# Joined: an alignment with blocks two slots apart and its teacher rows loaded early, and expert picks and most normalised rows made in the attention's tail

## The reference, cut to what matters

```python
x = x + _L0_xattn_ref(_layernorm(x), ctx, ctx, ...)      # 16 heads of 16, softmax attention
x = x + _L0_ffn_ref(_layernorm(x), W1, b1, W2, b2, Wr, br)  # mixture of 8 experts, top 1
x = x + _L1_xattn_ref(ctx, _layernorm(x))                # dynamic time warping (below)
x = x + _L1_ffn_ref(...)
x = x + _L2_xattn_ref(...)                               # attention
x = x + _L2_ffn_ref(...)                                 # mixture of 8 experts, top 2
x = x + _L3_xattn_ref(...)
x = x + _L3_ffn_ref(...)

# experts: logits = x @ Wr + br, the expert is their argmax, the gate a softmax of them
# warping, for each of 8 batches (teacher = ctx rows, student = normalised x rows):
D = sqrt(max(aa + bb - 2 * a @ b.T, 0))                  # 256 x 256 distances
R[i, j] = D[i, j] + min(R[i-1, j], R[i, j-1], R[i-1, j-1])
# walk back from R[255, 255] to R[0, 0] by the least neighbour;
# expanded[j] = sum of the teacher rows i that the path pairs with j
```

## Time and profile before

| | |
|---|---|
| median of 3 runs | 2441.24 us (2434.01 to 2441.58) |
| the profiled execution's own time | 2440.11 us |
| its span in the profile | 2438.3 us |
| busy: PE / PEld / DVE | 1987.9 (82%) / 1621.2 (66%) / 1604.2 (66%) |
| busy: ACT / POOL | 1183.1 (49%) / 951.7 (39%) |
| mean granted clock of PE | 0.825 |

### The profile page before, as it was taken

One profiled execution on the slowest core, in us unless ns is written; L12 is line 12 of the kernel. 1 busy time (PEld: TensorE's weight loads), 2 busy tenths in 40 slices (PEclk: granted clock), 3 DMA queues, 4 the chain that ended last, 5 costly groups with the idle time before them and its releaser, 6 DMA issues. The chain is left out here.

```text
span 2438.3 us, 40723 instructions
## 1 busy us (share of the span) xinstructions
PE 1987.9 (82%) x13441; PEld 1621.2 (66%) x13441; DVE 1604.2 (66%) x5274; ACT 1183.1 (49%) x3293; POOL 951.7 (39%) x919
## 2 busy tenths in 40 slices
PE   8985999599948967976999947777878778777888
PEld 5663898499937855655999935566656666665555
DVE  6776111588974237854111168999999999995786
ACT  3544232455421115543333325687777787875444
POOL 3311454300007023303555425666666666662210
PEclk9997999655779989987999965577777678757899
DMA  3112565520315012315354330000000000101442
GB/s 97 62 47 84 205 240 177 150 37 1 108 48 182 0 65 74 101 36 184 130 205 161 106 123 25 1 31 18 31 18 31 31 1 31 49 1 63 164 157 77
DMA packets 101861, 204.50 MB, mean 84 GB/s; under 512 B 20158, under 2 KB 70550, under 8 KB 93718
## 3 DMA queue, kind: packets, MB, share of 16 engines
q1 hardware_dynamic: 77568, 116.19, 14.3%
q0 software_dynamic: 23808, 85.50, 10.2%
q10 hardware_dynamic: 280, 0.23, 0.0%
HBM read 216.24 MB, written 55.28 MB: 111 GB/s over the span
## 5 line engine op out<-in xcount | busy, mean ns | idle before, releaser
L833 DVE MATCH_REPLACE8 l3a_left<-l3a_top,l3a_left 128x256 f32<-128x256 f32 x768 | 308.3, 409 | 0.0
L826 DVE MAX8 l3a_top<-l3a_left 128x8 f32<-128x256 f32 x768 | 285.5, 413 | 0.0
L525 POOL TENSOR_TENSOR l3a_prob<-l3a_expd,l3a_rest 128x512 f32<-128x512 f32 x128 | 162.8, 1272 | 211.4 <-ACT l3a_rest L608 210.4
L363 PEld LDWEIGHTS l3a_psO<-l3a_probT,l3a_vp 128*128 128x128 f32 x1024 | 185.5, 269 | 69.7 <-ACT l3a_probT L624 40.6
L363 PE MATMUL l3a_psO<-l3a_probT,l3a_vp 128*128 128x128 f32 x1024 | 210.0, 370 | 24.7 <-ACT l3a_probT L624 24.6
L345 PE MATMUL l3a_psT<-all_ident,l3a_prob 128*128 128x128 f32 x512 | 112.8, 361 | 106.0 <-POOL l3a_prob L525 105.2
L512 POOL TENSOR_TENSOR l3a_kept<-l3a_raw_sc,l3a_mone 128x512 f32<-128x512 f32 x128 | 163.7, 1279 | 71.9 <-ACT l3a_raw_sc L592 67.9
L2043 ACT ACTIVATE l2f_hT<-l2f_psH,l2f_wt 128x128 f32<-128x128 f32 x312 | 89.2, 369 | 209.8 <-PE l2f_psH L1997 209.8
L518 POOL TENSOR_TENSOR l3a_sc_sb<-l3a_kept,l3a_mlow 128x512 f32<-128x512 f32 x128 | 164.1, 1282 | 10.0
L345 PEld LDWEIGHTS l3a_psT<-all_ident,l3a_prob 128*128 128x128 f32 x512 | 80.0, 186 | 123.9 <-POOL l3a_prob L525 123.4
L2403 PE MATMUL dtw_psS<-dtw_r,all_shift 128*128 128x1 f32 x596 | 152.7, 356 | 10.2 <-DVE dtw_r L2583 9.8
(11 more groups left out here) (599 smaller groups left out, 4730.4 us busy)
## 6 DMA issues: line engine op xcount, KB each, us to landing
key_at<-l3a_a_k SPq DMA_DIRECT2D x8, 768.0 KB, 3.3
kv_at<-dtw_vd SPq DMA_DIRECT2D x8, 512.0 KB, 2.8
k_at<-dtw_kx SPq DMA_DIRECT2D x8, 512.0 KB, 4.2
l1f_kx<-k_at SPq DMA_DIRECT2D x8, 512.0 KB, 4.5
kv_at<-l1f_k SPq DMA_DIRECT2D x8, 512.0 KB, 3.2
l2a_k<-kv_at SPq DMA_DIRECT2D x8, 512.0 KB, 5.6
...
```

The costliest lines, as they stand in the source:

```text
L363: mm = nc.tensor.matmul(psO[y % 2][:, c, 0:P], vp[:, p, kc, c, g * P:g * P + P], probT[:, u % 2, kc, e, :], start=(j == 0 and e == 0 and k ...
L525: nc.gpsimd.tensor_tensor(prob[:, u % 4, :, :], expd[:, u % 2, :, :], rest[:, u % 2, :, :], ALU.subtract).then_inc(picked, 1)
L826: ins = nc.vector.max(top[:, e, eight], rows[:, e, :] if r else scores[:, e, :])
L833: ins = nc.vector.match_replace(out=rows[:, e, :], in_to_replace=top[:, e, eight], in_values=rows[:, e, :] if r else scores[:, e, :], imm_ ...
```

## The change

Five parts; the diff is cut to its core.

1. Attention tail (`l0a`, `l2a`): `routed(5)` is done before `out_project(6)` instead of after `values_apart(15)`, with two "spare" places in the bank order. ACT takes the roots there, in two groups (tiles 0 to 11, 12 to 15), and makes 12 of the 16 tiles of normalised rows; DVE makes `rstd`, the offsets and the picks of 12 tiles and then of 4; SP writes three of the four groups to `rows_x`.
2. `moe`: the roots, `max`, `max_index` and logits are gone from its start; `hot` is DVE's first work, four tiles of rows are left; two gathers are issued before the fourth fetch; 2 `keep_busy` instead of 4.
3. `Teacher`: the teacher rows (2 MB) and four turned batches (1 MB) are loaded during `l0f`, behind block 1's row copy, and their squares made on ACT behind the gelus of blocks 8 to 15.
4. `alignment`, front: moments in three groups (4, 4, 8 tiles), `minus_two(0)` and `(1)` before the third; no clearing of all of `d` and `r`; four `d2` buffers; 2 `keep_busy` at PE's start.
5. `alignment`, loop: `LAG` = 2, so `SLOTS` = 286. The scan takes its start value straight from PSUM, where PE's product is added onto columns that hold the large number for the first block; ACT is out of the loop. The scan writes 17 elements (row 0 of `r` too).

```diff
@@ paired_attention: turns, banks, PE
-                weighed = [("out", B - 2)] + weighed
+                weighed = ([("fl", B - 3), ("spare", 0), ("spare", 1)] if route is not None else []) + [("out", B - 2)] + weighed
...
-                if at >= 8:
-                    pe.wait_ge(reader[turns[at - 8][0]], turns[at - 8][1] + 1)
+                last = at - 8
+                if last >= 0 and turns[last][0] == "spare":
+                    last -= 8
+                if last >= 0:
+                    pe.wait_ge(reader[turns[last][0]], turns[last][1] + 1)
...
                 if y == 2 * B - 1 and t == 1:
+                    if route is not None:
+                        routed(B - 3)
                     out_project(B - 2)
@@ ACT
+            def row_roots(i):
+                a, z = PICKS[i]
+                act.wait_ge(r_moments, z)
+                nc.scalar.activation(r_std[:, a:z], mv[:, a:z, 1], ACT.Sqrt, bias=r_eps[:, 0:1]).then_inc(r_rooted, 1)
+            def rows_normalised(a, z):
+                for n in range(a, z):
+                    nc.scalar.activation(route["xn"][:, n, :], x[:, n, :], ACT.Identity, bias=route["offset"][:, n:n + 1],
+                                         scale=rstd[:, n:n + 1]).then_inc(r_norm, 1)
...
+                if route is not None and n == NQ + 5:
+                    act.wait_ge(r_eps_set, 1)
+                    row_roots(0)
+                if route is not None and n == NQ + 11:
+                    row_roots(1)
+                if route is not None and n == NQ + 9:
+                    rows_normalised(8, PICKS[0][1])
                 if route is not None and t == 3 and 0 <= (n - 15) // 4 < B:
                     read_rows((n - 15) // 4)
+                if route is not None and n == NQ + 6:
+                    act.wait_ge(r_off, 1)
+                    rows_normalised(0, 8)
@@ DVE
+            def row_scales(i):
+                a, z = PICKS[i]
+                dve.wait_ge(r_rooted, i + 1)
+                then(nc.vector.reciprocal(rstd[:, a:z], r_std[:, a:z]))
+                nc.vector.scalar_tensor_tensor(out=route["offset"][:, a:z], in0=mv[:, a:z, 0], scalar=-1.0, in1=rstd[:, a:z],
+                                               op0=ALU.mult, op1=ALU.mult).then_inc(r_off, 1)
+            def pick_experts(i):
...
+                dve.wait_ge(lg_ev, z // QT)
...  (lg * rstd, + br, max and max_index of tiles a to z)
+                if route is not None and n == NQ + 13:
+                    pick_experts(1)
                 if n == NQ + 7:
+                    if route is not None:
+                        row_scales(0)
                     normalise_apart(APART + 1)
...
                     if route is not None:
                         row_moments(B - 1)
+                        dve.wait_ge(r_in, 32)
+                        pick_experts(0)
+                        row_scales(1)
@@ moe
-            keep_busy(nc, psX[:], ident, 4)
+            keep_busy(nc, psX[:], ident, 2)
...
             act.wait_ge(eps_set, 1)
-            nc.scalar.activation(std[:], mv[:, :, 1], ACT.Sqrt, bias=epst[:, 0:1]).then_inc(rooted, 1)
+            for t in range(LATE, NT):
+                nc.scalar.activation(xn[:, t, :], x[:, t, :], ACT.Identity, bias=offset[:, t:t + 1], scale=rstd[:, t:t + 1]).then_inc(x_norm, 1)
...
+                if early and early.FROM <= j < early.FROM + B:
+                    early.squares(act, j - early.FROM)
...
             fetch(0, 1)
+            pool.wait_ge(kept.sem, kept.base + 64)
+            pool.wait_ge(put_set, 1)
+            gather(0)
+            gather(1)
             fetch(1, 1)
-            pool.wait_ge(kept, 64)
-            pool.wait_ge(put_set, 1)
-            for j in range(4):
-                gather(j)
+            gather(2)
+            gather(3)
@@ Teacher
+    FROM = 8
+    def load(self, sp):       # SP of l0f, after pe has turned blocks 0 and 1 (b_read 2)
+        sp.dma_start(self.ctx_sb[:], self.ctx.rearrange("b (t p) d -> p (b t) d", p=P)).then_inc(self.ctx_in, 16)
+        for b in range(4):
+            self.load_turned(sp, b)
@@ alignment
-LAG = 3
+LAG = 2
-        stats = RowStats(s, nc, x, rstd, nmean, negative=True)
+        stats = RowStats(s, nc, x, rstd, nmean, negative=True, cuts=(4, 8, NT))
-        d2 = s.sb("d2", [P, 2, QT, S])
+        d2 = s.sb("d2", [P, 4, QT, S])
...
+            keep_busy(nc, psS[0][:], ident, 2)
             turn(0)
...
+            for p in range(2):
+                nc.tensor.matmul(psS[p][:, 0:SLOTS], ident[:], consts["outside"][:].to_broadcast([P, SLOTS]), start=True, stop=False,
+                                 skip_group_check=True)
             for t in range(LAG, SLOTS):
                 pe.wait_ge(step, t - LAG + 1)
-                if t >= LAG + 2:
-                    pe.wait_ge(passed, t - LAG - 1)
-                nc.tensor.matmul(psS[t % 2][:, 0:1], consts["shift"][:], r[:, WB, 2 + t - LAG:3 + t - LAG],
-                                 start=True, stop=True).then_inc(moved, 1)
+                nc.tensor.matmul(psS[t % 2][:, t:t + 1], consts["shift"][:], r[:, WB, 2 + t - LAG:3 + t - LAG], start=False,
+                                 stop=(t >= SLOTS - 2), skip_group_check=True).then_inc(moved, 1)
...
-            act.wait_ge(corner, 2)
-            for t in range(LAG, SLOTS):
-                act.wait_ge(moved, t - LAG + 1)
-                nc.scalar.activation(r[:, 0, 2 + t:3 + t], psS[t % 2][:, 0:1], ACT.Identity,
-                                     bias=consts["outside"][:, 0:1], scale=1.0).then_inc(passed, 1)
...
                 dve.wait_ge(near_set, t + 1)
                 if t >= LAG:
-                    dve.wait_ge(passed, t - LAG + 1)
-                nc.vector.tensor_tensor_scan(r[:, 1:1 + WB, 2 + t], near[:, t % 2, :], d[:, :, t], r[:, 0, 2 + t:3 + t],
+                    dve.wait_ge(moved, t - LAG + 1)
+                    above_first = psS[t % 2][:, t:t + 1]
+                else:
+                    above_first = r[:, 0, 2 + t:3 + t]
+                nc.vector.tensor_tensor_scan(r[:, 0:1 + WB, 2 + t], near[:, t % 2, :], d[:, :, t], above_first,
                                              ALU.min, ALU.add).then_inc(step, 1)
```

More of the change, by code:

```diff
@@ L126, in roots @@
     def roots(self, act):
-        for g in range(2):
+        for g in range(len(self.cuts) - 1):
             self.root(act, g)
@@ L2162, in _ @@
             ins.then_inc(hot_done, 1)
+            nc.vector.memset(ones[:], 1.0)
+            nc.vector.tensor_scalar(tile_no[:], c["iota"][:, 0:KT], 1.0, None, ALU.add)
+            then(nc.vector.tensor_scalar(spare[:], c["iota"][:, 0:NB], float(P), c["lane"][:, 0:1], ALU.mult, ALU.add))
+            then(nc.vector.tensor_scalar(spare[:], spare[:], float(P + KT * P), None, ALU.add))
+            if k_top == 1:
+                nc.vector.tensor_tensor(lg2[:], lg[:], top[:, :, 0:1].to_broadcast([P, NT, E]),
+                                        ALU.subtract).then_inc(exp_in, 1)
+            else:
+                nc.vector.tensor_tensor(lg2[:, :, 0], top[:, :, 1], top[:, :, 0], ALU.subtract).then_inc(exp_in, 1)
             dve.wait_ge(ranked, 1)
@@ L2565, in _ @@
             minus_two(0)
+            minus_two(1)
+            stats.moments(dve, 2)
             for b in range(B):
-                if b + 1 < B:
+                if 2 <= b + 1 < B:
                     minus_two(b + 1)
                 squared(b)
-            dve.wait_ge(corner, 2)
+            dve.wait_ge(corner, 4)
             for t in range(SLOTS):
@@ L2601, in _ @@
             nc.vector.tensor_tensor(dg[:, :, 1:], above_left, above, ALU.is_le)
-            then(nc.vector.tensor_tensor(above_min[:], above, above_left, ALU.min))
-            nc.vector.tensor_tensor(left[:, :, 1:], above_min[:], beside, ALU.is_gt)
+            then(nc.vector.tensor_tensor(above_min, above, above_left, ALU.min))
+            nc.vector.tensor_tensor(left[:, :, 1:], above_min, beside, ALU.is_gt)
             then(nc.vector.tensor_tensor(uz[:, :, 1:], dg[:, :, 1:], down_at[:].unsqueeze(1).to_broadcast([P, CH, SLOTS]), ALU.add))
@@ L2903, in program @@
-        gated_ffn(nc, "l1f", x, ident, rstd, mean, t["L1_gate"], t["L1_up"], t["L1_down"], k_at, kv_at, (t["c_cos"], t["c_sin"]), t["c_even"])
-        paired_attention(nc, "l2a", x, ident, rstd, mean, t["c_even"], 1.0,
-                         weights("L2_", {k: k for k in ("wq", "wo")}), o_at, rope=(t["c_cos"], t["c_sin"]), kv_at=kv_at,
-                         route={**route, "wr": t["L2_wr"]})
-        moe(nc, dma, "l2f", 2, x, ident, rstd, consts, route, t["L2_br"], (t["L2_table1"], t["L2_table2"]), rows_x, rows_y)
+        with ExitStack() as hold:
+            route["xn"] = hold.enter_context(nc.sbuf_tensor("l0_rows", [P, NT, D], F32))
+            paired_attention(nc, "l0a", x, ident, rstd, mean, t["c_even"], DK ** -0.5,
+                             weights("L0_", {k: k for k in ("wq", "wk", "wv", "wo", "bq", "bk", "bv", "bo")}), o_at, ctxT=t["ctxT"],
```

(12 more changed lines are left out.)

213 lines of the change are left out of this document (107 added, 106 removed).

## The result

| | before | after |
|---|---|---|
| median of the runs | 2438.89 us (4 runs) | 2405.52 us (4 runs, 2404.66 to 2406.74) |
| ratio | | 0.9864, 95% interval 0.985 to 0.9877 |
| the profiled execution's own time / span | 2440.11 / 2438.3 us | 2406.74 / 2405.0 us |
| granted clock, mean | 0.825 | 0.831 |

What follows compares the result with a forecast made beforehand. No engine bounds the whole; each layer's own chain does: PE mid-expert-layer, DVE in the warping loop. Terms -10.1 - 7.4 - 5 - 7.0 - 2.7 = -32.2 us give 2407.9 profiled, median 2409; 8-in-10 range 2398 to 2427.

Steps and rivals of the forecast that it cites:

- The tail: End of `l0a` and `l2a`: fl(5) earlier gains 4.3 us, later picks cost 2.7, net -1.6 in `l0a`; net -2.4 in `l2a`.
- `l0f` and `l2f`: Expert layer starts: `l0f` -8.5 us (hot -6.3, gather -3.2, up(0) +1); `l2f` -5.0, with up(0) +1.7.
- the reason given, idle PE ahead of up(0): Expert layer starts: shortened keep_busy leaves PE idle, so up(0) runs slower, +1 us in `l0f`, +1.7 in `l2f`.
- The front: Warping before its loop: fewer moment tiles, no clearing and a higher clock start distances earlier, -5 us (bounds -1.5 and -7).
- the 1 us of the four buffers: End of the warping's front: four buffers save about 1 us.
- a loss that didn't come: Warping's front: later turned rows can give back as much as the four buffers save, about 1 us.
- The loop: Warping loop: 15 slots fewer at 0.507 us save 7.6 us, the 17th scan element costs 0.6, net -7.0.
- The rival of a dearer start value: Warping loop: PSUM start value or round trip lengthens slots; 67 ns a scan costs 19 us, giving 2428; chance 0.2 together.
- The rivals' loops: Warping loop: 156.2 us with a round trip of 0.84 (chance 0.2 with dearer start), 200.5 at 1.15 (turning over, 0.04).
- The round trip: Warping loop: scan through PE to the scan two slots on takes 0.74 us, against 0.762 available; fits by 0.02.
- turn over: Warping loop: PE and DVE alternate on one bank, every slot waits a whole round trip; up to +53 us, 2462; chance 0.04.
- Behind the loop: After the warping loop: DVE works over 286 columns instead of 301, 5% less, -2.7 us.

## Why the prediction was right

- **The tail**: PE's order was DVE's hold-up, as said; gain and cost were both under-sized (5.1 and 3.4 measured, 4.3 and 2.7 forecast) and cancel. That the net came out is luck.
- **`l0f` and `l2f`**: hot 6.4 us sooner (6.3), the gather 3.3 sooner (3.2), up(0) +0.8 and +1.6 for the shortened dummy products (+1 and +1.7). The price of the shorter filler was real and avoidable; the reason given, idle PE ahead of up(0), is only part of it: in `l0f` of the trace after, two dummy products no longer bring the clock up at all.
- **The front**: -7.2 against -5. Of the 2.2 us missed, 0.8 lie ahead of the second distances: the clock was full through all of the first ones (1.97 us), not from their middle, and the second begin 3.1 us behind them instead of 3.8. And I had set the 1 us of the four buffers against a loss that didn't come: from the last distances to the loop it is 10.8 us instead of 12.1.
- **The loop**: the step that failed is "15 x 0.507 less, and +2 ns for the 17th element". A slot costs 13 ns more, not 2: 2 for the 17th element, 5 for the start value in PSUM and some 6 for the near. Of these 6, row distance and place of the output explain about 4 together; the rest stays open. 286 x 0.011 = 3.1 us of the 3.2 missed. The rival of a dearer start value was right in kind and thirteen times too dear: 5 ns, not 67. By the rule of the Trainium skill (VectorE: DVE Perf Modes, the cycle table under the TRN2 errata) it would be an estimated 65 ns. The measured 5 ns decide against it for a start value. The rivals' loops (156.2 and 200.5 us) are slots alone and leave out the some 2 us of pauses that the 147.5 hold, so they were priced some 2 us too cheap.
- **The round trip** was forecast to fit by 0.02 us, and it fits; the loop doesn't turn over. The slot that came out 13 ns longer itself left more room: 0.78 us instead of 0.76.
- **Behind the loop**: the long operations lost 5% each (5.18 to 4.93 us); DVE's part to the walk is 2.3 us shorter, and the rest 0.4 longer, which was not followed up.

So the sum, 32.2 forecast and 33.4 measured, holds two errors of opposite sign, 3.2 us in the loop and 2.2 in the front, and 1.6 us of layers that nobody touched. The mechanisms are the forecast ones, save a part of the clock's in `l0f`; that the sum is met within 1.2 us is in part luck.
